# Softmax attention on one core: products for the maxima on 64 rows, the value block at the end of a period, the maxima turned in float16

## The reference, cut to what matters

```python
# x: (8, 512, 128) float32; 16 heads of 64; scale = 64 ** -0.5
x = x + 0.5 * ffn0(layernorm(x))
q, k, v = (split_heads(layernorm(x) @ W.T) for W in (Wq, Wk, Wv))
sim = einsum('bhid,bhjd->bhij', q, k) * scale
m = max(sim, axis=-1, keepdims=True)
e = exp(sim - m)
attn = e / (sum(e, axis=-1, keepdims=True) + 1e-10)
x = x + (einsum('bhij,bhjd->bhid', attn, v) merged over heads) @ Wo.T + bo
...
```

## Time and profile before

| | |
|---|---|
| time, median of 3 runs | 2273.55 us (2270.85 to 2274.36) |
| the profiled execution: time | 2278.47 us |
| the profiled execution: span | 2276.7 us |
| mean granted TensorE clock | 0.931 |
| busy: PE, VectorE, ScalarE, POOL | 82%, 73%, 47%, 47% |
| attention, from the first score product to the last addition to x | 268 to 1154 us of the span |

### The profile page before, as it was taken

The page is one execution under the profiler, slowest core; times in us unless marked ns, Lnnn a source line. Parts: engine busy times, 40 slices in busy tenths (PEclk is TensorE's granted clock), DMA queues, the critical chain, the costliest instruction groups (busy, mean ns, idle before and its releaser), DMA issues. The chain is left out here.

```text
span 2276.7 us, 36764 instructions
## 1 busy us (share of the span) xinstructions
PE 1866.1 (82%) x12205; PEld 1097.1 (48%) x12205; DVE 1669.5 (73%) x3322; ACT 1066.1 (47%) x2294; POOL 1080.2 (47%) x1304
## 2 busy tenths in 40 slices
PE   0555489999999999999935548999948888789999
PEld 0334234444444444444414435666637677656665
DVE  5887677888788877888778875666667777746665
ACT  0112255555555555555511135555537667445555
POOL 0111255555555555555611134555545556345555
PEclk9888599999999999999968977999979999879999
DMA  6000122222222222222100000000000000000000
GB/s 181 0 0 1 28 56 63 61 59 56 60 60 61 57 57 62 60 61 57 43 0 1 0 1 1 1 0 0 0 0 1 1 1 1 1 1 9 9 9 9
DMA packets 77058, 64.53 MB, mean 28 GB/s; under 512 B 12224, under 2 KB 75904, under 8 KB 76928
## 3 DMA queue, kind: packets, MB, share of 16 engines
q1 hardware_dynamic: 71392, 57.41, 9.9%
q10 hardware_dynamic: 5536, 5.52, 0.8%
HBM read 10.32 MB, written 2.10 MB: 5 GB/s over the span
## 5 line engine op out<-in xcount | busy, mean ns | idle before, releaser
L795 ACT ACTIVATE at_pT<-at_turned 128x512 f32<-128x512 f32 x512 | 305.6, 597 | 292.2 <-PE at_turned L862 273.3
L1022 POOL TENSOR_TENSOR m_g<-m_gT,m_g 128x512 f16<-128x512 f32 x260 | 301.4, 1159 | 232.1 <-ACT m_g L1005 232.1
L1036 PE MATMUL m_h<-m_xT,m_w 128*128 (+1 forms) x1572 | 386.8, 383 | 19.9 <-PEq L463 19.9
L694 DVE TENSOR_REDUCE at_nmax<-at_score 128x1 f32<-128x512 f32 x512 | 337.2, 680 | 71.8 <-PE at_score L839 68.7
L673 POOL TENSOR_TENSOR m_w_attn<-at_pT 128x512 f32<-128x512 f32 x128 | 162.4, 1269 | 377.1 <-ACT at_pT L795 377.1
L972 DVE TENSOR_TENSOR m_gT<-m_silu,m_h 128x512 f32<-128x512 f32 x262 | 180.3, 688 | 200.5 <-ACT m_silu L1001 200.4
L1001 ACT ACTIVATE m_silu<-m_h 128x512 f32<-128x512 f32 x262 | 156.6, 598 | 227.1 <-PE m_h L1036 227.1
L716 DVE RECIPROCAL m_w_attn<-m_w_attn 128x512 f32<-128x512 f32 x64 | 214.6, 3353 | 38.6 <-ACT m_w_attn L801 38.6
L900 PE MATMUL at_pv<-at_pT,at_v 128*64 128x512 f32 x1024 | 231.4, 594 | 0.0
L1055 PEld LDWEIGHTS m_y<-m_w,m_g 128*128 128x128 f16 x3072 | 192.9, 98 | 60.5
L1036 PEld LDWEIGHTS m_h<-m_xT,m_w 128*128 128x128 f16 x1572 | 144.3, 99 | 149.6 <-issue 28.3
(11 more groups left out here) (231 smaller groups left out, 3262.6 us busy)
## 6 DMA issues: line engine op xcount, KB each, us to landing
at_both<-at_part_q SPq DMA_DIRECT2D x128, 128.0 KB, 2.4
at_kh<-at_part_k SPq DMA_DIRECT2D x256, 64.0 KB, 2.0
at_both<-at_part_q SPq DMA_DIRECT2D x128, 64.0 KB, 2.0
at_kl<-at_part_k SPq DMA_DIRECT2D x128, 64.0 KB, 2.0
m_x<-in_x SPq DMA_DIRECT2D x8, 256.0 KB, 4.7
at_both<-at_mrow SPq DMA_DIRECT2D x128, 1.0 KB
out_x<-m_x SPq DMA_DIRECT2D x8, 256.0 KB, 2.3
m_wqkv<-in_w_qkv ACTq DMA_DIRECT2D x1, 1152.0 KB, 6.6
```

The costliest lines, as they stand in the source:

```text
L694: nc.vector.tensor_reduce(nmax[head][:, qt:qt + 1], score[use % 2][:], AX.X, ALU.max, negate=True)\
L795: nc.scalar.activation(pT[g % 2][:, head, kt, :], turned[i % 2][:], ACT.Exp).then_inc(exp_done, 1)
L1022: nc.gpsimd.tensor_tensor(g16[u % 4][:, 1, :], gT[u % 4][:], g16[u % 4][:, 0, :], ALU.subtract).then_inc(low_done, 1)
L1036: last = nc.tensor.matmul(bank[:], mem["w12_16"][:, w_part, e, first:first + P], mem["xT"][:, x_part, ds(b * SEQ, SEQ)], start=(i == 0), s ...
```

## The change

The scores for the maxima are no longer made from the copies in `both` and `kh` but from `part` itself, which has two sets now: two heads, each on its own 64 rows (`halves`), one product after the other, into the two banks `score[0]` and `score[1]`. A call of `scores` makes the products of both heads for one query tile. The maxima of both heads go to one float16 tile `nmax`, are turned once a period by a float16 matmul with `ident16` into the bank `sums`, copied once as 8 rows, and put in place by two DMAs. In PE's list `max_turned`, `output`, `values` and the projection of v stand at the end of the period. The lists of VectorE, ScalarE and SyncE are reordered. q and k are scaled down by 4 and 16, and the exponential scales by 64. `vv` has three buffers instead of four, `oT` one instead of two. The bodies that were removed from `scores`, `max_turned`, `neg_max` and the two `max_row` stand in the code above and are left out of the diff.

```diff
-        M_UNIT = 64.0
+        SHRINK = 64.0
+        SCALES = (DH ** -0.5 / W_ATTN / 4.0, 1.0 / W_ATTN / 16.0)
...
-        part = [s.sb(f"part_{n}", [P, 2, SEQ], F16) for n in "qk"]
-        vv = [s.sb(f"v{i}", [P, TPB, P]) for i in range(4)]
+        part = [[s.sb(f"part_{n}{i}", [P, 2, SEQ], F16) for n in "qk"] for i in range(2)]
+        vv = [s.sb(f"v{i}", [P, TPB, P]) for i in range(3)]
...
+        nmax = s.sb("nmax", [P, P], F16)
+        ident16 = s.sb("ident16", [P, P], F16)
+        mrow = s.sb("mrow", [UPP, P], F16)
+        oT = s.sb("oT", [P, SEQ])
...
+                def max_row(g):
+                    sp.wait_ge(m_out, g + 1)
+                    for head in range(2):
+                        sp.dma_start(both[g % RING][DH:DH + 1, 1, head, :].rearrange("o (t q) -> o t q", q=P),
+                                     mrow[head * TPB:(head + 1) * TPB, :]).then_inc(m_in, 16)
 
...
                         to_rows(g + 2, 0, 0)
                         sp.wait_ge(lo_done, 2 * (g + 2) + 1)
                         to_rows(g + 2, 0, 1)
-                    if live(g + 1):
-                        max_row(g + 1, 0)
-                    if live(g + 2):
                         sp.wait_ge(hi_done, 2 * (g + 2) + 2)
                         to_rows(g + 2, 1, 0)
+                    if live(g + 1):
+                        max_row(g + 1)
+                    if live(g + 2):
                         sp.wait_ge(lo_done, 2 * (g + 2) + 2)
                         to_rows(g + 2, 1, 1)
 
...
+                    qt, head = divmod(i, 2)
+                    col = head * TPB + qt
+                    dve.wait_ge(s_done, UPP * g + i + 1)
+                    nc.vector.tensor_reduce(nmax[:, col:col + 1], score[head][:], AX.X, ALU.max, negate=True).then_inc(s_read, 1)
+                def max_row(g):
+                    dve.wait_ge(m_done, g + 1)
                     if g:
-                        dve.wait_ge(m_in[head], 16 * g)
-                    nc.vector.tensor_scalar(mrow[head][:], score[use % 2][0:TPB, 0:P], 1.0 / M_UNIT, None, ALU.mult)\
-                      .then_inc(s_read, 1)
+                        dve.wait_ge(m_in, 32 * g)
+                    nc.vector.tensor_copy(mrow[:], sums[0:UPP, 0:P]).then_inc(m_out, 1)
...
-                    if g >= 2:
-                        dve.wait_ge(out_done, g - 1)
-                    nc.vector.tensor_tensor(oT[g % 2][:], pv[:], rinv, ALU.mult).then_inc(o_done, 1)
+                    if g:
+                        dve.wait_ge(out_done, g)
+                    nc.vector.tensor_tensor(oT[:], pv[:], rinv, ALU.mult).then_inc(o_done, 1)
 
...
                 for g in PERIODS:
                     if live(g + 1):
                         neg_max(g + 1, 0)
                         neg_max(g + 1, 1)
-                    if live(g):
-                        max_row(g, 1)
+                    if live(g - 2):
+                        normalise(g - 2)
                     if live(g + 1):
                         neg_max(g + 1, 2)
                         neg_max(g + 1, 3)
                     if live(g + 2):
                         low(g + 2, 0)
                     if live(g + 1):
-                        max_row(g + 1, 0)
+                        neg_max(g + 1, 4)
+                        neg_max(g + 1, 5)
+                        neg_max(g + 1, 6)
+                        neg_max(g + 1, 7)
+                        max_row(g + 1)
                     if live(g + 2):
                         low(g + 2, 1)
                     if live(g - 1):
                         inv_total(g - 1)
-                    if live(g + 1):
-                        neg_max(g + 1, 4)
-                        neg_max(g + 1, 5)
-                    if live(g - 1):
-                        normalise(g - 1)
-                    if live(g + 1):
-                        neg_max(g + 1, 6)
-                        neg_max(g + 1, 7)
                     if live(g - 2) and (g - 2) % PAIRS == PAIRS - 1:
                         add_x((g - 2) // PAIRS)
 
...
                 def high(g, which):
 
                     act.wait_ge(proj_done, 3 * g + 1 + which)
-                    if g:
-                        act.wait_ge(s_in[(g - 1) % RING], 16 * S_DMAS * ((g - 1) // RING + 1))
-                        act.wait_ge(t_in[(g - 1) % RING], 16 * T_DMAS * ((g - 1) // RING + 1))
-                    scale = (DH ** -0.5 / W_ATTN, 1.0 / W_ATTN)[which]
-                    nc.scalar.mul(part[which][:, 0, :], proj[:], scale).then_inc(hi_done, 1)
+                    if g >= 2:
+                        act.wait_ge(s_done, UPP * (g - 1))
+                        act.wait_ge(t_in[(g - 2) % RING], 16 * T_DMAS * ((g - 2) // RING + 1))
+                    scale = SCALES[which]
+                    nc.scalar.mul(part[g % 2][which][:, 0, :], proj[:], scale).then_inc(hi_done, 1)
 
...
-                    nc.scalar.activation(pT[g % 2][:, head, kt, :], turned[i % 2][:], ACT.Exp).then_inc(exp_done, 1)
+                    nc.scalar.activation(pT[g % 2][:, head, kt, :], turned[i % 2][:], ACT.Exp, scale=SHRINK)\
+                      .then_inc(exp_done, 1)
 
...
-                        exp(g, 2)
                     if live(g + 2):
                         high(g + 2, 0)
                     if live(g):
+                        exp(g, 2)
                         exp(g, 3)
+                        exp(g, 4)
+                        exp(g, 5)
                     if live(g + 2):
                         high(g + 2, 1)
+                    if live(g):
+                        exp(g, 6)
+                        exp(g, 7)
                     if live(g - 1):
                         total_out(g - 1)
-                    if live(g):
-                        for i in range(4, 7):
-                            exp(g, i)
                     if live(g + 2):
                         values_in(g + 2)
-                    if live(g):
-                        exp(g, 7)
 
...
+                def scores(g, qt):
+                    if g and qt == 0:
+                        pe.wait_ge(s_read, UPP * g)
+                    elif qt:
+                        pe.wait_ge(s_read, UPP * g + 2 * qt)
+                    if qt == 0:
+                        pe.wait_ge(lo_done, 2 * g + 2)
+                    q, k = part[g % 2]
+                    for head in range(2):
+                        nc.tensor.matmul(score[head][:], q[halves[head], 0, qt * P:(qt + 1) * P], k[halves[head], 0, :],
+                                         start=True, stop=True).then_inc(s_done, 1)
+                def max_turned(g):
+                    pe.wait_ge(s_read, UPP * (g + 1))
+                    if g:
+                        pe.wait_ge(m_out, g)
+                    if g >= 3:
+                        pe.wait_ge(total_done, g - 2)
+                    nc.tensor.matmul(sums[:, 0:P], nmax[:], ident16[:], start=True, stop=True).then_inc(m_done, 1)
 
...
-                    if kt == 0:
-                        pe.wait_ge(m_in[head], 16 * (g + 1))
+                    if i == 0:
+                        pe.wait_ge(m_in, 32 * (g + 1))
...
                     pe.wait_ge(added, 2 * (g + 1))
                     if g:
                         pe.wait_ge(total_done, g)
+                    pe.wait_ge(m_out, min(g + 3, PAIRS_ALL))
...
                 pe.wait_ge(set_up, RING + 3)
                 for g in PERIODS:
                     for i in range(UPP):
-                        if live(g + 1):
-                            scores(g + 1, i)
+                        if i % 2 == 0 and live(g + 1):
+                            scores(g + 1, i // 2)
                         if live(g):
                             scores_turned(g, i)
-                        if i == 1 and live(g):
-                            max_turned(g, 1)
-                        if i == 2 and live(g + 2):
+                        if i == 1 and live(g + 2):
                             project(g + 2, 0)
-                        if i == 3:
-                            if live(g - 2):
-                                output(g - 2)
-                            if live(g + 2):
-                                project(g + 2, 1)
-                            if live(g + 1):
-                                max_turned(g + 1, 0)
-                            if live(g - 1):
-                                values(g - 1)
-                        if i == 6 and live(g + 2):
-                            project(g + 2, 2)
+                        if i == 5 and live(g + 2):
+                            project(g + 2, 1)
+                    if live(g + 1):
+                        max_turned(g + 1)
+                    if live(g - 2):
+                        output(g - 2)
+                    if live(g - 1):
+                        values(g - 1)
+                    if live(g + 2):
+                        project(g + 2, 2)
```

(42 more changed lines are left out.)

52 lines of the change are left out of this document (16 added, 36 removed).

## The result

The kernel after takes 2282.57 us (median of five, 2281.64 to 2285.65) against 2273.2 (median of five; the first three gave 2273.55): the ratio is 1.0046, interval [1.0031, 1.0061], so 9.4 us slower. A second series gave 1.0047 [1.0033, 1.0061]. I had forecast 21.6 us slower (2295): the direction and the mechanism hold, the size is less than half.

What follows compares the result with a forecast made beforehand. PE was taken as the bound, with 12.8 of work in 13.46 us. Legs of 7.60 plus 6.25 gave 13.85, 0.39 longer; 63 periods make 24.6, less 3: 21.6 on 2273.55, so 2295 us, range 2258 to 2322.

Steps and rivals of the forecast that it cites:

- The two-bank wait: On PE, each score pair waits until both maxima of the pair before are read, holding everything behind it.
- legs 2 and 4: Stretches from one score pair to the next without a projection: VectorE path 1.83 us against PE's 1.32.
- The main rival: Attention stage: old overlap of maxima and products goes on, period 0.75 us less, 2223 us; chance 0.05.
- a switch costs 0.10 and 0.09: PE changing between 64-row pairs and full-size products: 0.10 us going out, 0.09 going in, taken from column rows.
- free switches: PE changes to and from row pairs at no cost: period 13.32, 2262 us; chance 0.21.
- serial pairs: A pair's products don't run side by side: 2322 us with switches paid, chance 0.10; 2279 with none, 0.05.
- That weighing's 13.98: Period in us if each change of tiling mode drains TensorE, laying bare a matmul's whole tail of 0.16; 2304 us.
- The price of a pair: Two score products on 64 rows hold PE 0.22 + 0.05 + 0.10 = 0.37 us; their maximum starts 0.48 after.
- The tail: PE alone at the period's end: turn of maxima, output, sums and pv, v projection, last switch; 6.25 us.
- `add_x` just fits: On VectorE, every eighth period, the addition fits between the reciprocal and the next first maximum, costing nothing.
- The start: zero: Stage start: first scores wait less for copies, first scores_turned wait more; net zero.
- The end: 3 us gained: Last period: values of the pair before (4.45) cover the 2.60 us wait of sums for POOL; about 3 us saved.

Runs made afterwards that it cites:

- e2: Kernel after, each maximum reading only 256 of the 512 keys; 2223.88 us, 0.9766 of the kernel before.
- e4: Kernel after, two of the four tiles of output moved from the period's end to after the fourth scores_turned; 2260.19 us, 0.9924 of the kernel before.
- e8: Kernel after, output split between legs 2 and 4 and the maxima turned into score[0] instead of sums; 2227.05 us, 0.9786 of the kernel before.
- e6: Kernel after with nmax in float32, turned by the float32 transpose; 2286.37 us, 1.0051 of the kernel before.
- e5: Kernel before with add_x moved ahead of the maxima row of head 0 in VectorE's list; 2273.41 us, 0.9983 of the kernel before.
- b2: Kernel before, unchanged, one more run with a second profile; 2276.32 us.
- a2: Kernel after, unchanged, run and profiled once more; 1.0047 of the kernel before.
- e7: Kernel after with output and values moved back to after the fourth scores_turned, total_out and reciprocal along; 2501.03 us, 1.0994 of the kernel before.
- e1: Kernel after with score products again on 128 rows, from the copies in both and kh; 2280.37 us, 1.0015 of the kernel before.
- e11: Kernel after with score products on 128 rows, the same kernel run again beside the kernel after; 2282.39 us, 1.0030 of the kernel before.

## Why the prediction was right or wrong, point by point

- *The two-bank wait makes legs 2 and 4 a round trip of VectorE, and the PE time saved turns into idle time.* The first half is right, and shown: the wait rows above, e2, e4 and e8. The second is right only in part: the idle time grew by 0.42, but most of the 1.0 saved went into the switches, which the prediction had in its legs as well. The main rival (PE stays the bound, 2223) fell: with PE's work unchanged, e2 took 64 us off.
- *The pairs run side by side, and a switch costs 0.10 and 0.09.* Right. The rivals of free switches and of serial pairs both fell by rows. The rule of the Trainium skill (TensorEngine Tiling, Key Properties, that a change of tiling mode drains) agrees in kind with 0.09 to 0.10 a switch; the whole tail of 0.16, which I had set against it, was too much. (That weighing's 13.98 gives 2303, not 2304. And the slices with PE at 9 begin at 342 us, not 320; nothing rests on either.)
- *The price of a pair, 0.37, and its maximum 0.48 behind.* Mis-sized: 0.32 and 0.42. The 0.05 by which the first pair of sums was longer does not belong to 64-row fp16 pairs. The four legs are 7.42 instead of 7.60. The tail is 6.33 instead of 6.25: `output` holds 1.04 (0.98 forecast), and e6 shows the 0.05 of that to go with the float16 turn ahead of it. Together the period is 13.75, not 13.85: 63 x 0.10 = 6 us of the miss.
- *`add_x` just fits.* True of the kernel after but for 0.05; its cost in the kernel before, seven periods of 13.95, was taken as nothing, since 13.46 was used for all 63. Another 3 us, shown by e5.
- *The start: zero.* Wrong: 2.4 us against an ordinary execution of the kernel before, 5.1 against the one that was first profiled. Close to 1 us more comes from counting the first two periods and the last among the steady ones. *The end: 3 us gained*: it was 0.8 (1.8 less the 1.0 of the last period).
- In the stage, 21.6 - 6.1 - 3.1 - 2.4 - 0.9 + 2.2 = 11.3, as b2 and a2 measure it. With the first execution of the kernel before the same sum gives 8.5. That the times differ by 9.4 and not by 11.3 comes from the code behind the stage and is not a success of either sum.
- The step that failed is the sum of the small terms, around a right mechanism: the pair priced at 0.37 with its maximum at 0.48 (measured 0.32 and 0.42), `add_x` in the old order put at nothing (3.1 us), and the start put at zero (2.4 us). The net of 0.3 us a period is a difference of two sums of 13, so a few hundredths in a term weigh much.
- *The value block at the end*: costed right as part of the tail, but for the 0.05 above. That it covers the row copies, I had as a margin; e7 shows what is under it.

## What to carry to other kernels

When two products share one emptying of their banks, ask what the consumer's round trip is (here 0.42 + 1.29 + 0.06) and how much of the engine's work stands inside it; halving the products only widens the gap, and the gain lies in moving other work into it (28 us for half of it, 59 for both). Array tiles pay only where their switches are few: here one slot of 0.22 saved cost 0.19 of switches, and undoing it made the period 0.10 shorter. For a change worth a few tenths of a per cent, look in the old trace also for its rare long periods and its start, since the new order may remove them by the way, and profile each kernel twice: here one late copy at the start moved the difference of the two stages from 11.3 to 8.4 us.

## What the runs showed of the hardware that was not expected

- Pairs on 64 rows have a switch price on PE, but none in latency: the reader starts 0.42 after the pair, as after a full product (0.42 in e1).
- After waits of 1.0 and 1.4 us close behind one another in every period (e7), PE fell to the lower level, 1.2 GHz, for the following 3 us (mean clock 0.53 from 716 to 719 us), in most of the periods, with a mean clock of 0.90 from 400 to 1300 us.
- A float32 product behind a float16 one held 0.05 more than behind a float32 one (`output` behind the turn, 1.04 against 0.99 in e6).
- The same code behind the stage took 1118 to 1127 us in different executions (1120 and 1127 in e1 and e11, the same kernel), and the first four periods of the stage differed by 2.8 between two executions of the kernel before, 1.5 of it one wait for a DMA.
